# A two-layer graph network on one core: a ring of eight chunks, and the edge MLP, products, transposes and clearing rearranged

## The chip, the cores and the metric

The kernel runs on 1 core of one Trainium2 chip. The metric is the device time in microseconds (us); lower is better. Each kernel was executed three times, and the median counts. One more execution was taken by the hardware profiler; its page and trace are what is read here.

## The reference

12500 nodes with 32 features each; 212500 edges, sorted by destination, each with a source, a destination, 32 edge features and 4 spherical coefficients.

```python
h = relu(layernorm(x))
x = x + gcn(h)            # h * norm_src, gather by src, sum by dst, * norm_dst, @ weight + bias, relu
h = relu(layernorm(x))
x = x + edge_layer(h)

def edge_layer(node_attr):                     # MUL = 8
    h = relu(edge_feat @ W1 + b1)              # [e,32] @ [32,64]
    w = (h @ W2 + b2).reshape(e, 4, 8, 8)      # [e,64] @ [64,256]
    s, v = node_attr[:, :8], node_attr[:, 8:].reshape(n, 8, 3)
    s_e, v_e = s[src], v[src]
    m0 = ALPHA * (einsum('ei,eio->eo', s_e * sh0, w_000) + C110 * einsum('eim,em,eio->eo', v_e, sh1, w_110))
    m1 = ALPHA * (einsum('ei,em,eio->eom', s_e, sh1, w_011) + einsum('eim,eio->eom', v_e * sh0, w_101))
    return segment sums of m0, m1 by dst + SI_SCALE * (s @ si_w0, v by si_w1)
```

## The kernel before

Edges are cut into chunks of 1024 (CHUNK: eight tiles of 128), 208 chunks in all. Both layers run over all chunks. Buffers of a chunk lie in a ring of RING = 4 slots (idx, sh, ef, and g for the gathered rows), and every engine's loop body covers one turn of the ring. The order on each engine is written out by hand, and semaphores tie the engines together.

The first 32 chunks (EARLY) are gathered from x_rows while VectorE and TensorE count degrees by one-hot products (L743, L501). Then table1 is written, and GpSimd gathers the other 176 chunks from it, eight indirect DMAs a chunk (L351), one for each tile.

Layer 1 (`beside_early`, then `alone`): a chunk's gathered rows are multiplied on TensorE with a one-hot of the destinations (`segment_sums`, L517) into a window of 68 columns, which VectorE adds into acc_a (`add_sums`, L800). In `beside_early`, a unit of the early chunks stands beside each two others; it goes from TensorE to VectorE and back for the source norms (L542, L862). In `alone`, once per ring turn (j == LOOK) `next_block` finishes a block of 512 nodes if its sums are complete: `mid_block` stages them (L918), multiplies by the weight (L572), normalizes, and ScalarE stores the rows to table2. There are 25 blocks. GpSimd may refill a slot once VectorE has made a one-hot that stands three units on (L788).

Between the layers, TensorE transposes all blocks (L591), four at a time, for ScalarE to copy into acc_b; GpSimd has cleared acc_b (L385) and VectorE clears acc_a (L952).

Layer 2 (`layer2`, `steps`, `products`): per chunk, TensorE makes the hidden layer in two halves of 512 edges (`hidden`, L610), ScalarE applies relu (L455) and the coefficients (`coefs`, L467), TensorE makes 256 weights per edge (`weights`, L622) into four PSUM banks, and VectorE multiplies weights by coefficients (L981, L986, L992), sums part of them (L997), finishes the messages (L1006), adds the sums of the chunk before (L800), and makes the next one-hot. TensorE sums the messages (L517). SyncE's loop waits, per chunk, for `hidden_psum`, then `gathered`, then `messages_ready`, and issues ef, idx and sh for four chunks ahead. GpSimd waits for idx and for the slot:

```python
over_iterations(pool, lambda i: gather(
    i, table2, i + ITERS, lambda c, j: wait(pool, d_ready, c - RING + 1)))
```

VectorE's order in layer 2 is: products(c, 1), join_sums(c - 1), finish_messages(c), d_coefs(c + 1), products(c + 1, 0).

## Time and profile before

| what | value |
|---|---|
| device time, median of 3 | 5982.73 us (5958.65 to 6010.7) |
| profiled execution, span from first to last instruction | 5914.9 us |
| the profiled execution's own device time | not listed; only its span is |
| mean granted TensorE clock | 0.696 of full |
| TensorE matmul / VectorE / ScalarE / GpSimd busy | 3299.9 / 2809.8 / 710.4 / 3294.7 us |

PE is TensorE, PEld its weight loads, DVE VectorE, ACT ScalarE, POOL GpSimd, SP SyncE. A timeline row is start in us, length in us, engine, line, operation, what it writes and reads, and in brackets the idle time of the engine ahead of it with what ended it. "remote" says that the release came from something that the profile can't name; "issue" that the engine waited for nothing that the profile shows. Times of single instructions are in ns in the tables of groups.

### The profile page before, as it was taken

Reading aid. Unit: us, or ns where it says so; the run is one execution under the profiler, and the core shown is the slowest. Engines: PE = TensorE matmul, PEld = TensorE weight load, DVE = VectorE, ACT = ScalarE, POOL = GpSimd, SP = SyncE. Lnnn points to the kernel's source line nnn. Section 1 sums busy time; section 2 is a strip of 40 time slices with the busy share of each in tenths; the row PEclk is TensorE's granted clock in tenths of the full one; section 3 lists DMA queues with packets and bytes.
Section 4 is the critical chain, followed back from the end, with each engine's and each line's share of the span. In section 5 each row is a group of like instructions: output and inputs, shape, how many; then the busy total and the mean of one; then the engine's idle time right before and its main releaser. Section 6 shows DMA issues by size and latency. Waiting matters only on the chain.

```text
span 5914.9 us, 64171 instructions
## 1 busy us (share of the span) xinstructions
PE 3299.9 (56%) x17022; PEld 2418.7 (41%) x17023; DVE 2809.8 (48%) x4667; ACT 710.4 (12%) x2399; POOL 3294.7 (56%) x3337
## 2 busy tenths in 40 slices
PE   7943333321112112111587877677878777787877
PEld 5733333321111111111355555454555555555545
DVE  7743333321111111111466666666666666666666
ACT  0000000000000000000322222222222222222222
POOL 7775555555555455566555555555555555555453
PEclk9996555555555555555778777878777777777787
DMA  1011111110000000000111111111111111111110
GB/s 41 11 32 28 30 28 28 31 21 11 11 11 11 10 11 11 11 11 11 20 21 20 20 20 20 20 21 20 20 20 20 20 19 20 20 19 20 19 20 14
DMA packets 224089, 113.87 MB, mean 19 GB/s; under 512 B 148848, under 2 KB 212145, under 8 KB 223953
## 3 DMA queue, kind: packets, MB, share of 16 engines
q0 software_dynamic: 106496, 54.74, 7.0%
q1 hardware_dynamic: 106281, 39.22, 3.0%
q10 hardware_dynamic: 11280, 19.53, 1.0%
q8 instruction: 15, 0.25, 0.0%
q14 instruction: 17, 0.14, 0.0%
HBM read 108.30 MB, written 4.92 MB: 19 GB/s over the span
## 4 chain that ended last, share of the span: by engine, by line
another core or an unknown queue 33%; PE 32%; issue 15%; DVE 8%; POOL 5%; DVEq 4%; ACT 2%; DMA 0%; ACTq 0%; POOLq 0%
PE ps L622 12%; PE ps L517 10%; PE ps L610 6%; POOL g L351 5%; DVEq L805 2%; PE ps L542 1%; DVEq L804 1%; ACT q L467 1%; PE ps L572 1%; PE ps L658 1%; PE ps L660 1%; ACT hid L455 1%; DVE prod_b L981 1%; DVE msg_b L997 1%
## 5 line engine op out<-in xcount | busy, mean ns | idle before, releaser
L351 POOL DMA_INDIRECT g<-table,idx x3072 | 2971.2, 967 | 2479.6 <-issue 922.9
L622 PE MATMUL ps<-w_s,hid 128*128 128x256 f32 x3328 | 1110.6, 487 | 365.6 <-ACT hid L455 322.0
L622 PEld LDWEIGHTS ps<-w_s,hid 128*128 128x128 f32 x3328 | 761.5, 241 | 932.0 <-issue 406.3
L800 DVE TENSOR_TENSOR acc_a<-acc_a,ps 33x68 f32 (+1 forms) x416 | 91.2, 219 | 2201.0 <-remote 1949.1
L997 DVE TENSOR_REDUCE msg_b<-prod_b 128x128 f32<-128x1024 f32 x416 | 827.2, 1989 | 0.0
L517 PE MATMUL ps<-onehot,g 128*33 128x68 f32 x2816 | 340.0, 310 | 558.4 <-DMA g<-table,idx 296.1
L610 PE MATMUL ps<-ef,w_s 32*64 32x512 f32 x832 | 543.9, 734 | 42.2 <-issue 36.9
L455 ACT ACTIVATE hid<-ps,b_s 64x512 f32<-64x512 f32 x416 | 283.1, 681 | 2357.7 <-remote 1153.8
L517 PEld LDWEIGHTS ps<-onehot,g 128*33 128x33 f32 x2816 | 302.1, 170 | 587.1 <-issue 309.5
L981 DVE TENSOR_TENSOR prod_b<-ps,q 128x768 f32<-128x768 f32 x416 | 395.5, 951 | 274.8 <-remote 196.7
L517 PEld LDWEIGHTS ps<-onehot,prod_a 128*128 128x128 f32 x3328 | 455.1, 212 | 41.6 <-issue 10.2
L572 PE MATMUL ps<-w_l_s,ef 33*128 33x33 f32 x200 | 51.9, 422 | 730.8 <-DVE ef L918 529.7
L517 PE MATMUL ps<-onehot,prod_a 128*128 128x68 f32 x3328 | 443.3, 292 | 9.9 <-DVE msg_b L1006 6.5
L517 PE MATMUL ps<-onehot,msg_b 128*56 128x68 f32 x3328 | 297.4, 237 | 193.8 <-issue 192.9
L467 ACT ACTIVATE q<-g,sh 128x32 f32<-128x32 f32 x1664 | 372.7, 309 | 0.0
L542 PE MATMUL ps<-norm_src,hid 128*128 128x100 f32 x512 | 119.5, 428 | 437.7 <-DVE hid L833 342.1
L351 POOL DMA_INDIRECT g<-x_rows,idx x256 | 310.0, 1211 | 79.8 <-issue 77.7
L572 PEld LDWEIGHTS ps<-w_l_s,ef 33*128 33x128 f32 x200 | 48.5, 324 | 737.0 <-DVE ef L918 534.1
L501 PE MATMUL ps<-acc_b 128*128 128x100 bf16 x1664 | 314.3, 370 | 34.2 <-DVE acc_b L743 34.2
L517 PEld LDWEIGHTS ps<-onehot,msg_b 128*56 128x56 f32 x3328 | 242.2, 139 | 218.7 <-issue 202.5
L788 DVE TENSOR_TENSOR onehot<-iota_all,dst_rel 128x544 f32<-128x544 f32 x416 | 300.2, 722 | 52.0 <-issue 29.9
L430 ACT ACTIVATE root<-stat 128x4 f32<-128x4 f32 x50 | 10.3, 206 | 2412.9 <-DVEq L694 2412.9
(108 smaller groups left out, 2343.7 us busy)
## 6 DMA issues: line engine op xcount, KB each, us to landing
g<-table,idx POOLq DMA_INDIRECT x3072
ef<-edge_t SPq DMA_DIRECT2D x208, 128.0 KB, 2.3
ef<-src_rows ACTq DMA_DIRECT2D x31, 512.0 KB
idx<-src_chunks SPq DMA_DIRECT2D x416, 4.0 KB
g<-x_rows,idx POOLq DMA_INDIRECT x256
sh<-sh_chunks SPq DMA_DIRECT2D x208, 16.0 KB
table<-hn ACTq DMA_DIRECT2D x1, 1600.0 KB
table<-hn ACTq DMA_DIRECT2D x25, 64.0 KB
```

Of the source, the lines that this page charges most:

```text
L351: pool.indirect_dma_start(out=g[:, j, t, 0:FEAT], out_offset=None, in_=table, in_offset=bass.IndirectOffsetOnAxis(ap=idx[:, j, t:t + 1], a ...
L455: act.activation(hid[0:HID, h, :], ps[0:HID, H_BANK + h, :], ACT.Relu, bias=b1_s[:, 0:1]).then_inc(hidden_ready, 1)
L467: act.activation(q[:, j % 2, t, 8:40], g[:, j, t, 0:FEAT], ACT.Copy, scale=sh[:, j, t, 0:1])
L501: mm = pe.matmul(deg, oh_p[:, b, :, t], oh_r[:, b, :, t], start=False, stop=False, skip_group_check=True)
L517: mm = pe.matmul(ps[0:m, S_BANK + b, col:col + WIN], r, oh(t), start=(t == 0), stop=(t == TILES - 1))
L542: mm = pe.matmul(ps[:, W_BANK + t // 4, NR * (t % 4):NR * (t % 4 + 1)], early_p[:, P * t:P * (t + 1)], norm_src[:, :], start=True, stop=True)
L572: mm = pe.matmul(mid_ps[:, r, :], by_column(staged1)[:, r, :], w_l0_s[:, :], start=True, stop=True)
L610: pe.matmul(ps[0:HID, H_BANK + h, :], w1_s[32 * j:32 * j + 32, :], ef[32 * j:32 * j + 32, 512 * h:512 * h + 512], start=True, stop=True, t ...
L622: mm = pe.matmul(w_ps[h][:, t, :], hid[:, h, P * t:P * t + P], w2_s[:, :], start=True, stop=True)
L788: dve.tensor_tensor(onehot[:, b, :, :], iota_all[:, None, 0:WIN].to_broadcast([P, TILES, WIN]), dst_rel[:, bass.ds(c * TILES, TILES)][:, : ...
L981: dve.tensor_tensor(prod_b[:, h, :, 0:3, :].rearrange("p t m (i o) -> p t m i o", o=MUL), w[:, :, 128:192].rearrange("p t (i o) -> p t i o ...
L997: dve.tensor_reduce(msg_b[:, b, 4 * h:4 * h + 4, 0:32].rearrange("p t (g o) -> p t g o", o=MUL), prod_b[:, h, :, :, :].rearrange("p t g (i ...
```

## The change

The ring has eight slots, so each loop body covers eight chunks and there are 26 turns instead of 52; blocks are looked for at two places in a turn (LOOKS), and four early chunks stand beside eight others. Layer 2's slot is free for GpSimd after the last product of its chunk. The hidden layer is one product per chunk of 64 rows with a block-diagonal W1 (two edges' features above each other, 128 output rows). The weight products have 64 rows each, alternately in the upper and the lower half of the array; b2 comes in by bf16 products of ones with b2 split into three bf16 parts. W2's last two groups are stored transposed so that the summed index of the products lies innermost, and ScalarE writes the v coefficients already repeated (vq). VectorE makes one coefficient itself and finishes messages ahead of `join_sums`. The transposes go into `mid_block`; acc_a is cleared block by block there, and acc_b by VectorE in layer 1. SyncE's loop over early chunks now waits for all of them before it loads bounds and first sources.

```diff
-RING = 4
+RING = 8
+EARLY_PER = 4
+LOOKS = (1, 5)
...
-            with sp.Fori(0, EARLY_ITERS - 1) as i:
+            with sp.Fori(0, EARLY_ITERS) as i:
                 load1(i)
...
-            pool.wait_ge(added1, A_UNITS)
-            pool.memset(acc_b[:, :], 0.0).then_inc(acc_b_clear, 1)
...
-                i, table2, i + ITERS, lambda c, j: wait(pool, d_ready, c - RING + 1)))
+                i, table2, i + ITERS, lambda c, j: wait(pool, weights_used, 2 * (c - RING + 1))))
...
                 act.wait_ge(table2_ready, b + 1)
-                act.dma_start(block_rows(table2, b), block_columns(hn, b)).then_inc(table2_out, 16)
+                act.dma_start(block_rows(table2, b), hn_b).then_inc(table2_out, 16)
+                act.wait_ge(table2_out, 16 * b + 16)
+                act.wait_ge(turned, b + 1)
+                act.activation(by_column(acc_b[64:96, bass.ds(b * BLOCK, BLOCK)]),
+                               turn_ps.rearrange("f (r p) -> f r p", p=P), ACT.Copy).then_inc(staging_free, 1)
...
-                act.wait_ge(hidden_psum, 2 * (RING * i + j) + h + 1)
-                act.activation(hid[0:HID, h, :], ps[0:HID, H_BANK + h, :], ACT.Relu,
+                act.wait_ge(hidden_psum, RING * i + j + 1)
+                act.activation(hid[:, j % 2, :], ps[:, H_BANK + j % 2, :], ACT.Relu,
                                bias=b1_s[:, 0:1]).then_inc(hidden_ready, 1)
...
-                    act.activation(q[:, j % 2, t, 8:40], g[:, j, t, 0:FEAT], ACT.Copy, scale=sh[:, j, t, 0:1])
-                act.activation(q[:, j % 2, :, 40:48], g[:, j, :, 0:MUL], ACT.Copy).then_inc(coefs_ready, 1)
+                    ins = act.activation(
+                        vq[:, j % 2, t, :].rearrange("p (m o i) -> p m o i", m=3, i=MUL),
+                        g[:, j, t, MUL:FEAT].rearrange("p (m i) -> p m i", m=3)[:, :, None, :].to_broadcast(
+                            [P, 3, MUL, MUL]), ACT.Copy, scale=sh[:, j, t, 0:1])
+                ins.then_inc(coefs_ready, 1)
...
             def steps(i):
                 for j in range(RING):
-                    relu(*after(i, j, 1), 1)
+                    relu(*after(i, j, 2))
                     coefs(*after(i, j, 1))
-                    relu(*after(i, j, 2), 0)
...
                 mm.then_inc(mid_ready, 1)
+                pe.wait_ge(table2_ready, b + 1)
+                for r in range(BR):
+                    mm = pe.transpose(turn_ps[:, P * r:P * r + P], hn_b[:, r, :], ident[:, :])
+                mm.then_inc(turned, 1)
...
+                pe.matmul(ps[:, H_BANK + j % 2, :], w1_s[k:k + HID, :], ef[k:k + HID, j // 2, :],
+                          start=True, stop=True, tile_position=(k, 0)).then_inc(hidden_psum, 1)
...
-                for t in range(4):
-                    mm = pe.matmul(w_ps[h][:, t, :], hid[:, h, P * t:P * t + P], w2_s[:, :], start=True, stop=True)
+                for h in range(2):
+                    k = HID * h
+                    pe.matmul(ps[:, W_BANK + 2 * n + h, :], ones_b[k:k + HID, :], bias3[k:k + HID, :],
+                              start=True, stop=False, tile_position=(k, 0))
+                for u in range(2):
+                    for h in range(2):
+                        k = HID * h
+                        at = P * (2 * n + u)
+                        mm = pe.matmul(w_ps[n][:, 2 * h + u, :], hid[k:k + HID, j % 2, at:at + P],
+                                       w2_s[k:k + HID, :], start=False, stop=(u == 1), tile_position=(k, 0))
...
-                    hidden(*half(i, j, 3))
-                    weights(*half(i, j, 2))
-                    hidden(*half(i, j, 4))
-                    weights(*half(i, j, 3))
+                    hidden(*after(i, j, 2))
+                    weights(*after(i, j, 1), 0)
+                    weights(*after(i, j, 1), 1)
...
-                dve.tensor_copy(staged1, acc_a[0:FEAT + 1, bass.ds(b * BLOCK, BLOCK)]).then_inc(mid_go, 1)
+                sums = acc_a[0:FEAT + 1, bass.ds(b * BLOCK, BLOCK)]
+                dve.tensor_copy(staged1, sums).then_inc(mid_go, 1)
+                dve.wait_ge(mid_go, b + 1)
+                dve.sem_inc(sums_staged, 1)
+                dve.tensor_copy(sums, acc_b[0:FEAT + 1, 0:BLOCK]).then_inc(acc_a_clear, 1)
...
+            dve.memset(acc_b[0:64, :], 0.0).then_inc(acc_b_clear, 1)
...
-                dve.wait_ge(coefs_ready, c + 1)
+                dve.wait_ge(gathered[j], GATH * (i + ITERS + 1))
+                dve.wait_ge(sh_in[j], 16 * (i + 1))
+                dve.tensor_tensor(q[:, b, :, MUL:2 * MUL], g[:, j, :, 0:MUL],
+                                  sh[:, j, :, 0:1].to_broadcast([P, TILES, MUL]), ALU.mult)
...
                     msg_b[:, b, 4 * h:4 * h + 4, 0:32].rearrange("p t (g o) -> p t g o", o=MUL),
-                    prod_b[:, h, :, :, :].rearrange("p t g (i o) -> p t g o i", o=MUL),
+                    prod_b[:, h, :, :, :].rearrange("p t g (o i) -> p t g o i", i=MUL),
                     AX, ALU.add).then_inc(reduced, 1)
...
                     products(c, j, 1)
-                    if j == LOOK:
+                    finish_messages(c, j)
+                    if j in LOOKS:
                         final = final_blocks(dve, c - 1)
                     if not first:
                         join_sums(c - 1, 1 - b, *limits)
-                    finish_messages(c, j)
```

## Rows read from the trace of the kernel before

**Rows 1.** The first line of the profile's page.
```profile
span 5914.9 us, 64171 instructions
...
```

**Rows 2.** Stretches: us; PE, PEld, DVE, ACT, POOL busy us (instructions); clock, DMA share, GB/s.
```profile
...
391.00:1266.00 875.00, 279.26 (x1951) 261.30 (x1952) 265.11 (x519) 0.42 (x1) 496.78 (x513) 0.60 0.13 29
1266.00:2784.00 1518.00, 277.62 (x2043) 249.01 (x2042) 244.85 (x841) 9.46 (x46) 850.16 (x896) 0.52 0.08 11
2885.00:5914.00 3029.00, 2387.66 (x11189) 1639.59 (x11187) 1984.73 (x2978) 655.46 (x2274) 1590.13 (x1629) 0.77 0.11 20
...
```

**Rows 3.** Groups of layer 2, forms apart: count, busy us, mean ns, idle before.
```profile
...
L622 PE MATMUL ps<-w_s,hid 128*128 128x256 f32 x3309 | 1104.1, 487 | 365.6 <-ACT hid L455 322.0 <-issue 40.8 <-DVE prod_a L992 0.7
L997 DVE TENSOR_REDUCE msg_b<-prod_b 128x128 f32<-128x1024 f32 x415 | 825.2, 1989 | 0.0
...
L610 PE MATMUL ps<-ef,w_s 32*64 32x512 f32 x824 | 538.0, 733 | 42.2 <-issue 36.9 <-DVE prod_a L992 4.4
...
L467 ACT ACTIVATE q<-g,sh 128x32 f32<-128x32 f32 x1655 | 370.7, 309 | 0.0
...
L455 ACT ACTIVATE hid<-ps,b_s 64x512 f32<-64x512 f32 x412 | 280.4, 681 | 2351.4 <-remote 1153.8 <-PE ps L610 1039.1 <-issue 158.3
...
```

**Rows 4.** Waits in layer 2: us in total, times, longest.
```profile
...
ACT hid L455 <- remote: 1153.8, 118, 23.5
...
POOL g L351 <- DMA idx<-src_chunks: 748.3, 110, 11.8
...
DVE acc_a L800 <- remote: 465.4, 90, 11.6
...
```

**Rows 5.** Timeline of layer 2, a held stretch: start, us, instruction, idle before.
```profile
...
4060.39 1.01 PE L610 MATMUL ps<-ef,w_s 32*64 32x512 f32 x2 [0.74 <-issue]
...
4065.76 0.94 POOL L351 DMA_INDIRECT g<-table,idx  x1 [0.30 <-issue]
4069.00 0.68 ACT L455 ACTIVATE hid<-ps,b_s 64x512 f32<-64x512 f32 x1 [15.90 <-remote]
4069.06 0.23 DVE L800 TENSOR_TENSOR acc_a<-acc_a,ps 128x68 f32 x1 [9.13 <-remote]
...
4073.93 0.94 POOL L351 DMA_INDIRECT g<-table,idx  x1 [7.23 <-DMA idx<-src_chunks]
...
```

**Rows 6.** Timeline of layer 2, VectorE in a free stretch.
```profile
...
4093.05 0.35 DVE L1006 TENSOR_TENSOR msg_b<-msg_b,sh 128x192 f32<-128x192 f32 x1
...
4102.41 0.34 DVE L1006 TENSOR_TENSOR msg_b<-msg_b,sh 128x192 f32<-128x192 f32 x1
...
```

**Rows 7.** Timeline of layer 1, behind the early chunks.
```profile
...
1825.37 0.95 POOL L351 DMA_INDIRECT g<-table,idx  x1 [0.30 <-issue]
1830.32 0.22 DVE L800 TENSOR_TENSOR acc_a<-acc_a,ps 33x68 f32 x1 [33.99 <-remote]
1830.98 0.42 DVE L918 COPY ef<-acc_a 33x512 f32 x1 [0.44 <-DVE acc_a L800]
...
1842.51 0.94 POOL L351 DMA_INDIRECT g<-table,idx  x1 [16.19 <-DVE onehot L788]
...
```

**Rows 8.** Line L860: duration in ns, min/median/max.
```profile
...
L860 DVE TENSOR_REDUCE q<-prod_b x32: 985/986/987, 452.2 to 1298.8; 128x8 f32<-128x800 f32 x32
...
```

**Rows 9.** Timeline of the seam between the layers.
```profile
...
2818.54 1.89 PE L591 MATMUL ps<-ident,hn 128*32 128x128 f32 x8 [7.27 <-DVEq L938]
...
2821.45 10.78 DVE L952 MEMSET acc_a<- 128x12868 f32 x1 [3.02 <-issue]
...
2822.47 0.95 POOL L351 DMA_INDIRECT g<-table,idx  x1 [25.18 <-DMA table<-hn]
...
2872.58 3.67 PE L610 MATMUL ps<-ef,w_s 32*64 32x512 f32 x4
...
```

**Rows 10.** Waits from 36 to 345 us, where the degrees are counted.
```profile
...
DVE acc_b L743 <- PE ps L501: 90.2, 101, 0.9
...
```

**Rows 11.** DMA queues of the page: packets, MB, share of 16 engines.
```profile
...
q8 instruction: 15, 0.25, 0.0%
...
```

More of the change, by code:

```diff
@@ L154, in gnn_program @@
         early_mean = flat_q[:, TILES * (FEAT + 2):TILES * (FEAT + 3)]
+        flat_a = prod_a[:, :, :, :].rearrange("p b t k -> p (b t k)")
+        bias_raw, bias_left = flat_a[0:1, 0:HALF], flat_a[0:1, HALF:2 * HALF]
+        bias_parts = [flat_a[0:1, (4 + k) * (HALF // 2):(5 + k) * (HALF // 2)].bitcast(BF16) for k in range(3)]
         early_x = flat_q[:, TILES * (FEAT + 3):TILES * (2 * FEAT + 3)].rearrange("p (t f) -> p t f", f=FEAT)
@@ L583, in _ @@
             other_blocks(pe, blocks1, mid_block)
-            pe.wait_ge(table2_ready, BLOCKS)
-            for n in range(-(-NR // 4)):
-                wait(pe, turned_used, n - 1)
-                for r in range(4 * n, min(NR, 4 * n + 4)):
-                    k = (r - 4 * n) * P
-                    mm = pe.transpose(ps[0:32, S_BANK + n % 2, k:k + P], hn[:, r, :], ident[:, :])
-                mm.then_inc(turned, 1)
-            def half(i, j, ahead):
-                j, h = j + ahead // 2, ahead % 2
-                return i + j // RING, j % RING, h
@@ L599, in beyond, with after, hidden @@
-            def beyond(i, j, h):
+            def after(i, j, n):
+                return i + (j + n) // RING, (j + n) % RING
+            def beyond(i):
                 return isinstance(i, int) and i >= ITERS
-            def hidden(i, j, h):
-                if beyond(i, j, h):
+            def hidden(i, j):
+                if beyond(i):
                     return
-                k = 2 * (RING * i + j) + h
-                if h == 0:
-                    pe.wait_ge(ef_in[j], 16 * (i + 1))
-                wait(pe, hidden_ready, k - 1)
-                pe.matmul(ps[0:HID, H_BANK + h, :], w1_s[32 * j:32 * j + 32, :],
-                          ef[32 * j:32 * j + 32, 512 * h:512 * h + 512], start=True, stop=True,
-                          tile_position=(32 * j, 0)).then_inc(hidden_psum, 1)
@@ new lines, in hidden, with weights @@
+                wait(pe, hidden_ready, c - 1)
+                pe.matmul(ps[:, H_BANK + j % 2, :], w1_s[k:k + HID, :], ef[k:k + HID, j // 2, :],
+                          start=True, stop=True, tile_position=(k, 0)).then_inc(hidden_psum, 1)
+            def weights(i, j, n):
+                if beyond(i):
+                    return
+                c = RING * i + j
+                pe.wait_ge(hidden_ready, c + 1)
+                wait(pe, weights_used, 2 * c + n - 1)
+                for h in range(2):
+                    k = HID * h
+                    pe.matmul(ps[:, W_BANK + 2 * n + h, :], ones_b[k:k + HID, :], bias3[k:k + HID, :],
+                              start=True, stop=False, tile_position=(k, 0))
+                for u in range(2):
+                    for h in range(2):
+                        k = HID * h
+                        at = P * (2 * n + u)
+                        mm = pe.matmul(w_ps[n][:, 2 * h + u, :], hid[k:k + HID, j % 2, at:at + P],
+                                       w2_s[k:k + HID, :], start=False, stop=(u == 1), tile_position=(k, 0))
@@ L946, in _ @@
             dve.wait_ge(table1_out, 16)
+            dve.wait_ge(bias_in, 16)
+            dve.memset(acc_b[0:64, :], 0.0).then_inc(acc_b_clear, 1)
+            dve.tensor_scalar(w2_s[:, 0:64], w2_s[:, 0:64], float(ALPHA * C110), None, ALU.mult)
+            dve.tensor_scalar(w2_s[:, 64:256], w2_s[:, 64:256], float(ALPHA), None, ALU.mult)
+            dve.tensor_scalar(sel_b_s[64:96, :], sel_b_s[64:96, :], float(SI_SCALE), None,
+                              ALU.mult).then_inc(weights_scaled, 1)
+            dve.wait_ge(acc_b_clear, 1)
+            two = bias_raw.rearrange("a (u w) -> a u w", w=256)
+            dve.tensor_scalar(two[:, :, 0:64], two[:, :, 0:64], float(ALPHA * C110), None, ALU.mult)
+            link(dve.tensor_scalar(two[:, :, 64:256], two[:, :, 64:256], float(ALPHA), None, ALU.mult))
+            left = bias_raw
+            for k in range(3):
+                link(dve.tensor_copy(bias_parts[k], left))
+                if k < 2:
+                    link(dve.tensor_tensor(bias_left, left, bias_parts[k], ALU.subtract))
+                    left = bias_left
+            dve.sem_inc(bias_split, 3)
             with dve.Fori(A_ITERS, REG_ITERS - 1) as i:
@@ L951, in _ @@
             other_blocks(dve, blocks1, mid_block)
[L952 to L957 removed]
+            dve.wait_ge(acc_a_clear, BLOCKS + 1)
             def d_coefs(i, j):
@@ L1100 @@
     w2 = np.concatenate([np.asarray(L1_gnn_W2), np.asarray(L1_gnn_b2)[None, :]])
-    w2 = np.concatenate([w2[:, 3 * mm:], w2[:, :mm], w2[:, 2 * mm:3 * mm], w2[:, mm:2 * mm]], axis=1)
+    turn = [w2[:, k * mm:(k + 1) * mm].reshape(-1, MUL, MUL).transpose(0, 2, 1).reshape(-1, mm) for k in (2, 1)]
+    w2 = np.concatenate([w2[:, 3 * mm:], w2[:, :mm], *turn], axis=1)
+    w1 = np.zeros((2, 2, FEAT, 2, HID), np.float32)
+    w1[:, 0, :, 0, :] = np.asarray(L1_gnn_W1)
+    w1[:, 1, :, 1, :] = np.asarray(L1_gnn_W1)
     skip = np.zeros((FEAT, FEAT), np.float32)
```

194 lines of the change are left out of this document (98 added, 96 removed).

## The prediction, made before the change was run

> **What bounds the kernel now.** I read the stretches first, then the groups of layer 2, its waits, and two stretches of its timeline. Layer 2 takes 3029.0 of the 5914.9 us [rows 1, 2]. It has 208 chunks, so a chunk costs 14.56 us. No engine is busy that long: in the same row TensorE is busy 2387.7 us (11.5 a chunk), VectorE 1984.7 (9.5), ScalarE 3.2 a chunk, and GpSimd issues eight gathers of 0.95 us with 0.30 between them, 8 x 1.25 = 10.0 us a chunk [rows 2, 5]. So handovers set the pace. The held stretch shows which: TensorE's hidden-layer product begins at 4060.39 and takes 1.01 us, yet ScalarE, which waits for it, starts at 4069.00; VectorE's add of sums, held 9.13 us, starts at 4069.06. Both begin 2.3 us after GpSimd's last gather of the burst ended (4065.76 + 0.94) [rows 5]. In layer 1 the same: last gather ends 1826.3, the add starts 1830.32 after 33.99 us [rows 7]. So TensorE's signals reach the others late while a long burst of gathers runs. Waits marked "remote" are of this kind: 1153.8 us at ScalarE, 465.4 at VectorE's add [rows 4]. After the release, VectorE must finish messages, SyncE must load indices, and only then does GpSimd go on, 7.23 us after its last gather; such waits for indices are 748.3 us, 3.6 a chunk [rows 4, 5]. Where nothing is held, a chunk takes 4102.41 - 4093.05 = 9.4 us, VectorE's own work [rows 6]. It isn't gathers alone that hold TensorE: while the degrees are counted they run too, and VectorE's longest wait for TensorE there is 0.9 us [rows 10]. The mechanism is not shown, only its coincidence with bursts behind that stage.
>
> **Layer 2, part by part.**
> VectorE: the sum of the products, 2 a chunk, takes 1.99 us for 1024 elements read at a stride of eight floats. The change packs the summed index innermost. A packed sum of 800 elements takes 0.986 us [rows 8], 1.23 ns an element, so 1024 take at most 1.26. Saved: 2 x 0.73 = 1.5 us a chunk. The three product instructions keep their element counts, so I cost them at nothing. One multiplication of 64 elements is added, between 0.1 and 0.35 us; I take 0.2. VectorE: 9.5 - 1.5 + 0.2 = 8.2 us.
> TensorE: the hidden products, two of 32 rows a chunk, become one of 64. L610 is busy 538.0/208 = 2.6 us a chunk; half goes, 1.3. The weight products stay eight of 256 columns, but on 64 rows, alternating between the upper and lower half of the array. L622 is busy 1104.1/208 = 5.3 us [rows 3]; if two halves run together 2.65 goes, if not nothing. I take 1.5, since the trace has no pair. Four bf16 bias products of 512 columns are added. Between nothing and 4 x 0.65 (a busy L610 instruction, 538.0/824) = 2.6; I take 1.3, the middle, because a bf16 product is one instruction where an fp32 one is two (824 instructions for 416 products) [rows 3]. TensorE: 11.5 - 1.3 - 1.5 + 1.3 = 10.0, between 7.6 and 12.8.
> The Trainium skill, "TensorEngine Tiling (Array Packing)", section Key Properties, has tiles loading and multiplying in parallel, but a drain at each change of tiling mode. By the first TensorE would have 8.9 us, by the second about what it has now; no row shows either.
> ScalarE: one relu of 128 rows replaces two of 64, each 681 ns. The eight copies grow from 32 to 192 elements: by the slope from 309 ns at 32 to 681 at 512, 433 ns each [rows 3]. Beside a small copy that goes, about +1 us a chunk, and -0.7 from the relu. It stays under 4.5 us and has VectorE's 8 us of cover; without that cover it would cost 1 us a chunk, 208 us.
> Order: VectorE now finishes messages of chunk c before it waits for the sums of c-1. Behind the held add used to stand the messages, behind them SyncE's index load and TensorE's own sums. Also the relu now comes a whole chunk ahead of its use, where it used to be a half. ScalarE still waits for the relu ahead of the coefficients, so that hold remains.
> The ring: with eight slots the indices lie ready, so the 3.6 us a chunk of index waits go. What is late next is the slot. The rule changes from the vsh sum to the last product of the chunk, but seven chunks back instead of three. GpSimd's bursts thereby close up, which is what holds TensorE.
> The pace: a burst of k chunks lasts 10.0k us. Then 2.3 us until signals come, then VectorE needs between a third of a chunk and a whole one (2.7 to 8.2 us) to free a slot; I take 5.3. For k = 2 a chunk costs (20 + 7.6)/2 = 13.8, for k = 3 12.5. VectorE works 8.2 us a chunk, and the first 6 to 9 us of a burst are free as in rows 6. I take 12.9 us. Layer 2: 208 x (14.56 - 12.9) = -345 us. The bounds are GpSimd's 10.0 to 10.4 us below, and above no gain at all.
>
> **The seam.** The transposes take from 2818.54 to 2872.58, 54 us, and go into the block steps of layer 1 [rows 9]. Their cover in layer 1 is GpSimd, which is not delayed by them. What is late next is the gather: it starts at 2822.47, and a first chunk needs 10.0 us. Net -54 + 10 = -44 us. The clearing of acc_a (10.8 us, at 2821.45) already lay beside the transposes; without its move it would now cost 10.8.
>
> **Layer 1.** It is 875 + 1518 us [rows 2]. Behind the early chunks the cycle is a burst of 32 gathers (four slots, 40 us) plus 16.19 us until VectorE frees a slot [rows 7]. With eight slots TensorE finds more data ready when it is released. If five chunks pass a cycle instead of four, (50 + 16.2)/5 = 13.2 us against 14.05, -0.8 over some 112 chunks, -90 us; if still four, nothing. I take -60. Against it: a block step gains one copy of 33 x 512 (0.42 us, as its staging copy [rows 7]) with a link, 25 x 0.7 = 17 us; TensorE waits in each for the whole block before it may sum the next chunk, beside GpSimd, 0 to 60 us, I take 15. Clearing acc_b moves from GpSimd to VectorE, 10.8 us as acc_a's took [rows 9], with scalings and splitting some 6 more one time. SyncE's bounds and first sources now stand behind all 32 early chunks, not 28: 4 x 10.0 = 40 us later, most of it beside gathers that run anyway; 0 to 40, I take 12. Sum: -60 + 17 + 15 + 17 + 12 = 0, between -120 and +90.
>
> **Sum.** -345 - 44 + 0 = -389: span 5914.9 - 389 = 5526. The median of the runs, 5982.73, stands 67.8 us above the profiled span; the profiled execution's own time isn't listed, so I carry this difference unchanged: 5594, say 5590 us.
>
> **Rivals.**
> Gather pace: if shorter TensorE work and the looser order let the free stretches persist (9.4 us already beside nearly continuous gathers, rows 6), layer 2 runs at 10.4: 208 x 4.16 = -865, with the seam 5074 us. For it: a 9.4 us chunk exists. Against: layer 1's holds, where TensorE has little to do and still waits 34 us. Chance 0.17.
> Longer holds (the other side): no index wait breaks the bursts, k goes to 4. A cycle is 40 us, 2.3, then VectorE may do in the free 9 us one chunk and must do three of 8.2 behind, of which about 8 us lie in the next burst: 40 + 2.3 + 17 = 59.3, 14.8 a chunk, +50 us; the early stage, with its handovers to and fro for each early chunk, has 32 of them, each held by one such 2.3 us more, 875 + 70, and the seam gives 44 back: 6059 us. It decides from the point where bursts of 32 gathers are the rule in layer 2. For it: rows 7. Chance 0.11.
> Code: the loop bodies double. If they no longer stay in the engines' buffers, each turn fetches. The instruction queue with the larger packets carries 15 in the whole run [rows 11], fewer than the 52 turns, so now the loops' turns fetch nothing there. Price: 25 turns of layer 2 with a hold like the 7.23 to 9.13 us of rows 5, +180 to 230: 5800 us. Chance 0.12.
> The Trainium skill, "Runtime: NRT & Kernel Launch", section Instruction fetch mechanics, says that a taken branch out of the current two-page window stalls for a fetch. By that the present loops should fetch too; rows 11 speak against it.
> Only engine work counts: ring and order give nothing, VectorE's 1.3 us a chunk are -270, seam -44: 5670; part of the forecast's own spread.
>
> **How the numbers follow.** Forecast 0.60 (5300 to 5800), gather pace 0.17, code 0.12, longer holds 0.11. Likeliest: 5590. To hold 8 in 10 the range runs from 5170 to 5900: all of the forecast and the code case, and the upper part of the gather-pace case. The three runs lie within 0.9% of one another, so 1% is about what can be told from no change. Faster by over 1% (under 5923) 0.87, within 1% 0.05, slower 0.08.
>
> **What would show it.** In the profile after: the packed sum at 1.2 us; the weight products' busy time well under 5 us a chunk if halves pair; index waits gone from GpSimd's rows, slot waits in their place; bursts of 16 to 24 gathers in layer 2 with remote waits behind them; layer 2 beginning at about 2840 plus layer 1's change; few instruction packets. I am wrong if bursts are long and a chunk still costs 14 us or more, if TensorE is busy over 13 us a chunk, or if the holds vanish.

## The result and the profile after

The changed kernel took 6079.48 us (median of 4 runs, 6073.26 to 6092.49) against 5987.74 us for the old one (median of 4 here): ratio 1.017, 95% interval 1.012 to 1.022. It is slower by 1.2 to 2.2%; 5590 was forecast, with a range from 5170 to 5900. A second comparison, in another job (a job is one session of runs on one chip), gave 6064.29 against 5885.63, ratio 1.030 (1.026 to 1.034).

The page of the changed kernel, its span, the engines' busy time and the two instruction queues [rows 1, 11]:

```profile
span 6080.2 us, 63715 instructions
...
PE 3107.2 (51%) x17438; PEld 2423.4 (40%) x17439; DVE 2534.7 (42%) x4908; ACT 771.2 (13%) x1983; POOL 3251.2 (53%) x3334
...
q14 instruction: 207, 1.69, 0.1%
q8 instruction: 29, 0.48, 0.0%
...
```

Its stretches: early chunks, rest of layer 1, seam, layer 2 (columns as in rows 2):

```profile
391.00:1280.00 889.00, 262.27 (x1828) 245.15 (x1829) 256.20 (x502) 0.42 (x1) 492.30 (x513) 0.59 0.14 28
1280.00:2670.00 1390.00, 282.13 (x2196) 250.89 (x2193) 282.29 (x899) 34.08 (x69) 846.54 (x889) 0.55 0.09 13
2670.00:2740.00 70.00, 24.90 (x156) 19.02 (x156) 23.64 (x78) 7.68 (x17) 20.98 (x23) 0.60 0.13 25
2743.00:6072.00 3329.00, 2217.64 (x11572) 1656.59 (x11570) 1700.06 (x3178) 714.46 (x1861) 1578.84 (x1647) 0.66 0.10 18
```

Layer 2 takes 3329.0 us for 208 chunks, 16.0 us a chunk where it was 14.56 [rows 2], though VectorE is busy only 1700.06/208 = 8.2 us a chunk and TensorE 10.7. So everything lost lies in layer 2, and in waiting. The layer even begins earlier than it did. Timeline of the seam, against rows 9:

```profile
2720.48 2.08 PE L597 MATMUL ps<-ef,w_s 64*128 64x512 f32 x4
...
2722.01 0.95 POOL L350 DMA_INDIRECT g<-table,idx  x1 [42.61 <-DMA table<-hn]
...
```

The first hidden product comes at 2720.48, not 2872.58, and the first gather at 2722.01, not 2822.47. By the first of these, layer 1 and seam gave 152 us. Layer 2 from there to the span's end took 3359.7 us where it took 3042.3: +317. The sum is the +165 us between the two spans.

Groups of layer 2 (rows 3 are their counterparts) and its waits (rows 4):

```profile
L615 PE MATMUL ps<-w_s,hid 64*128 64x256 f32 x3298 | 897.0, 495 | 421.2 <-issue 414.4
...
L463 ACT ACTIVATE vq<-g,sh 128x192 f32<-128x192 f32 x1656 | 594.3, 446 | 6.5 <-issue 6.5
...
L1011 DVE TENSOR_REDUCE msg_b<-prod_b 128x128 f32<-128x1024 f32 x414 | 501.2, 1211 | 0.0
...
L597 PE MATMUL ps<-ef,w_s 64*128 64x512 f32 x410 | 331.4, 896 | 21.7 <-issue 21.6
L609 PE MATMUL ps<-bias,ones_b 64*128 64x512 bf16 x824 | 315.8, 484 | 200.5 <-issue 122.7 <-DVE prod_a L1006 75.7
```
```profile
ACT hid L451 <- remote: 2079.1, 100, 88.4
DVE acc_a L794 <- remote: 1159.5, 89, 64.0
POOL g L350 <- DVE prod_a L1006: 1126.9, 100, 21.8
```

The instructions cost about what was forecast. The waits don't: ScalarE's remote wait went from 1153.8 to 2079.1 us, VectorE's from 465.4 to 1159.5, and where GpSimd waited 748.3 us for indices it waits 1126.9 for a slot. One cycle of the changed kernel, out of its timeline (as rows 5):

```profile
4168.62 0.95 POOL L350 DMA_INDIRECT g<-table,idx  x1 [11.72 <-DVE prod_a L1006]
...
4176.83 0.97 PE L597 MATMUL ps<-ef,w_s 64*128 64x512 f32 x1
...
4177.02 0.36 DVE L1020 TENSOR_TENSOR msg_b<-msg_b,sh 128x192 f32<-128x192 f32 x1
...
4185.28 0.27 PE L510 MATMUL ps<-onehot,prod_a 128*128 128x68 f32 x1 [1.64 <-issue]
...
4187.41 0.27 PE L510 MATMUL ps<-onehot,prod_a 128*128 128x68 f32 x1 [1.85 <-issue]
4187.70 0.95 POOL L350 DMA_INDIRECT g<-table,idx  x1 [0.30 <-issue]
...
4191.73 0.69 ACT L451 ACTIVATE hid<-ps,b_s 128x512 f32<-128x512 f32 x1 [23.46 <-remote]
4191.79 0.23 DVE L794 TENSOR_TENSOR acc_a<-acc_a,ps 128x68 f32 x1 [14.41 <-remote]
...
4199.41 0.68 DVE L1006 TENSOR_TENSOR prod_a<-ps,q 128x512 f32<-128x512 f32 x1
...
4200.90 0.95 POOL L350 DMA_INDIRECT g<-table,idx  x1 [12.25 <-DVE prod_a L1006]
```

Sixteen gathers run from 4168.62 to 4188.65. Some ten us in, TensorE drops to an instruction every 0.7 to 2 us, for no cause that the profile shows ("issue"). Such a stretch, together with the late signals at its end, is called a hold below. The hidden product that ScalarE waits for ended at 4177.80; ScalarE starts at 4191.73, 3.1 us behind the last gather. VectorE had stopped at 4177.38. Then 9.1 us pass until GpSimd starts again (4191.79 to 4200.90): VectorE works its way to the product that frees a slot. 20.0 + 3.1 + 9.1 = 32.2 us for two chunks, 16.1 each.

### The profile page after: what moved, and what is told of

Its sections match the earlier page's. It is cut to its first block, busy times and chain, and to the rows that moved or that the text cites. A ratio compares the mean times of both kernels' runs of the same rounds, so it can differ in the third digit from the quotient of the medians.

```text
span 6080.2 us, 63715 instructions
## 1 busy us (share of the span) xinstructions
PE 3107.2 (51%) x17438; PEld 2423.4 (40%) x17439; DVE 2534.7 (42%) x4908; ACT 771.2 (13%) x1983; POOL 3251.2 (53%) x3334
## 4 chain that ended last, share of the span: by engine, by line
another core or an unknown queue 35%; PE 22%; issue 22%; DVE 9%; DVEq 5%; ACT 4%; POOL 4%; DMA 0%; ACTq 0%; POOLq 0%
PE ps L510 10%; PE ps L615 5%; ACT vq L463 4%; POOL g L350 4%; PE ps L597 2%; DVE prod_b L996 2%; DVEq L799 2%; PE ps L535 2%; DVEq L798 2%; DVE msg_b L1011 1%; PE ps L609 1%; PE ps L565 1%; DVE prod_a L1006 1%; DVE prod_b L1000 1%
## 5 line engine op out<-in xcount | busy, mean ns | idle before, releaser
L350 POOL DMA_INDIRECT g<-table,idx x3072 | 2941.3, 957 | 2660.3 <-DVE prod_a L1006 1126.9
L615 PE MATMUL ps<-w_s,hid 64*128 64x256 f32 x3328 | 903.7, 496 | 421.2 <-issue 414.4
L510 PE MATMUL ps<-onehot,prod_a 128*128 128x68 f32 x3328 | 626.2, 341 | 411.1 <-issue 399.1
L615 PEld LDWEIGHTS ps<-w_s,hid 64*128 64x128 f32 x3328 | 591.4, 246 | 613.2 <-issue 571.2
L510 PEld LDWEIGHTS ps<-onehot,prod_a 128*128 128x128 f32 x3328 | 587.8, 258 | 544.4 <-issue 508.1
L463 ACT ACTIVATE vq<-g,sh 128x192 f32<-128x192 f32 x1664 | 597.2, 446 | 15.8 <-DMA g<-table,idx 9.3
L996 DVE TENSOR_TENSOR prod_b<-ps,vq 128x768 f32<-128x768 f32 x416 | 396.4, 953 | 382.3 <-ACT vq L463 180.9
L1011 DVE TENSOR_REDUCE msg_b<-prod_b 128x128 f32<-128x1024 f32 x416 | 503.7, 1211 | 0.0
L451 ACT ACTIVATE hid<-ps,b_s 128x512 f32<-128x512 f32 x208 | 143.0, 688 | 2593.4 <-remote 2079.1
L609 PE MATMUL ps<-bias,ones_b 64*128 64x512 bf16 x832 | 318.3, 486 | 211.8 <-issue 133.1
L597 PE MATMUL ps<-ef,w_s 64*128 64x512 f32 x416 | 334.5, 897 | 21.7 <-issue 21.6
```

The costliest lines, as they stand in the source:

```text
L350: pool.indirect_dma_start(out=g[:, j, t, 0:FEAT], out_offset=None, in_=table, in_offset=bass.IndirectOffsetOnAxis(ap=idx[:, j, t:t + 1], a ...
L451: act.activation(hid[:, j % 2, :], ps[:, H_BANK + j % 2, :], ACT.Relu, bias=b1_s[:, 0:1]).then_inc(hidden_ready, 1)
L463: ins = act.activation(vq[:, j % 2, t, :].rearrange("p (m o i) -> p m o i", m=3, i=MUL), g[:, j, t, MUL:FEAT].rearrange("p (m i) -> p m i" ...
L510: mm = pe.matmul(ps[0:m, S_BANK + b, col:col + WIN], r, oh(t), start=(t == 0), stop=(t == TILES - 1))
L597: pe.matmul(ps[:, H_BANK + j % 2, :], w1_s[k:k + HID, :], ef[k:k + HID, j // 2, :], start=True, stop=True, tile_position=(k, 0)).then_inc( ...
L609: pe.matmul(ps[:, W_BANK + 2 * n + h, :], ones_b[k:k + HID, :], bias3[k:k + HID, :], start=True, stop=False, tile_position=(k, 0))
```

## The experiments

Each run is compared with the old kernel on the same chip in the same job. Runs of different jobs are best compared by ratio, since the old kernel itself took 5886 to 5988 us in the jobs with holds. The "pace" is my own figure, in us a chunk: start of the first gather of layer 2's chunk 192 less that of chunk 16, over 176. A burst ends where GpSimd gathers nothing for 1.5 us. The last two columns are for bursts of 16 gathers: how many of all bursts of these chunks they are, and VectorE's busy time inside one (mean, us; a burst is 20 us long). The last four rows come from jobs in which nothing was held (below).

```
run               us       before   ratio (95%)            pace   bursts of 16   VectorE in one
before            5987.7   -        -                      14.67  37 of 126      13.3
changed (2nd)     6064.3   5885.6   1.030 (1.026..1.034)   15.92  80 of 96       9.1
r1_ring4          5955.0   5885.6   1.011 (1.008..1.015)   15.67  69 of 107      8.8
f1_slot           5717.5   5897.1   0.969 (0.964..0.973)   14.24  60 of 116      11.0
f2_order          5855.9   5897.1   0.992 (0.988..0.995)   15.04  74 of 101      9.7
f3_nobias         6134.2   5897.1   (one run)              16.46  88 of 88       8.8
g4_slot_order     5797.3   5982.5   0.969 (0.967..0.972)   14.48  64 of 106      10.7
r1_pause1         5371.6   5897.1   0.910 (0.906..0.914)   12.66  0              -
g2_before_pause   5524.5   5982.5   0.923 (0.920..0.926)   12.60  0              -
g1_best           5293.3   5982.5   0.884 (0.882..0.886)   12.76  0              -
h1_memset2        5302.5   5895.4   0.898 (0.894..0.901)   12.71  0              -
h2_memset1        5228.5   5895.4   0.886 (0.882..0.889)   13.04  0              -
h3_every2         5542.7   5895.4   0.940 (0.935..0.945)   13.83  66 of 110      11.2
e1_ring4          4354.9   4372.8   0.996 (0.994..0.997)   10.24  no gap at all  -
e2_pause1         4863.5   4372.8   1.112 (1.110..1.114)   12.64  0              -
e2_pause2         5380.4   4372.8   1.231 (1.228..1.233)   15.18  0              -
h4_mixed          5020.1   4374.1   1.148 (1.146..1.150)   12.22  0              -
```

**First job: another state of the machine.** The ring of four, with everything else as changed:

```diff
-RING = 8; EARLY_PER = 4; LOOKS = (1, 5)   # and twelve UNITS
+RING = 4; EARLY_PER = 2; LOOKS = (1,)     # six UNITS
```


> The changed kernel with the ring set back to four chunks (two early chunks to a turn, one look for a finished block); products, bias, order of VectorE's steps, transposes and clearing stay as changed. Long bursts: with four slots the index loads again break up GpSimd's work in layer 2, as before the change, and VectorE keeps its 8.2 us a chunk: 13.3 to 14.2 us a chunk in layer 2 and 5600 to 5800 us. Code: the loop bodies halve, so the second queue's instruction packets fall from 207 to some 20 and the kernel again comes to 5600 to 5900 us; this run can't part the two. Products, bias or order at fault: 15.5 us a chunk or more in layer 2, 6000 us or more.

It took 4354.86 us, but the old kernel beside it took 4372.83 instead of some 5900: in this job nothing was held. Waits of e1_ring4 in layer 2:

```profile
ACT hid L450 <- PE ps L596: 586.0, 202, 9.0
POOL g L349 <- issue: 491.4, 1612, 0.3
```

No remote wait is left, and GpSimd gathers through layer 2 without a gap of 1.5 us. So whether there are holds depends on a state of the machine: the old kernel is the same program in both. It isn't a matter of the chip either: a chip on which the old kernel took 5885.63 us in one job had it at 4374.06 in a later one (h4_mixed's). What sets the state I don't know. Without holds e1_ring4 stands at GpSimd's 10.2 us a chunk and is 0.4% faster than the old kernel. The changed kernel itself was never caught there, and of the old one there is no trace without holds.

> The changed kernel; in layer 2 GpSimd stores one row of 32 floats by a DMA of its own into a scratch row ahead of each chunk's gathers, and waits until it has landed (some 2 us in which it gathers nothing). Long bursts: no burst of 16 is left without a gap; if a gap of 2 us lets TensorE's signals out, a chunk takes 12 to 13.5 us and the kernel 5250 to 5550 us; if the gap must be as long as the 3.1 us seen behind a burst, little changes. Code: GpSimd's pause changes nothing in the loops' back edges, 6080 us or more, up to 6500 if every pause adds to the chain (208 x 2 us).

> The same with two such small DMAs one behind the other ahead of each chunk's gathers, some 4 us. Long bursts: the gap is longer than the 3.1 us seen behind a burst, so every chunk's signals get out; a chunk takes 13 to 14.5 us, 5450 to 5800 us. Code: 6080 to 6900 us.

The edit of e2_pause1, in short (the two lines stand in layer 2 only):

```diff
 for j in range(RING):
+    pool.dma_start(scratch, x_rows[0:1, :]).then_inc(paused, 16)
+    pool.wait_ge(paused, 16 * (RING * i + j + 1))
     pool.wait_ge(idx_in[j], 16 * (iteration + 1))
```

With no holds to break, the pauses only cost: the pace is 12.64 and 15.18 us, and the time 491 and 1008 us over the old kernel's. These runs decide nothing on bursts. (e2_pause2 has two such pairs.)

**The ring, under holds.** c1_after is the changed kernel once more, the table's second row.

> The changed kernel, unchanged. In the runs just before, the old kernel took 4373 us, not the 5988 us beside which the changed one was first timed, and the remote waits were gone from the traces: whether TensorE's signals are held depends on more than the kernel. If this run falls where they are held, the changed kernel again takes 6080 us and the ratio is again 1.01 to 1.02. If it falls where they are not, GpSimd's gathers set the pace of both layers (10.0 to 10.3 us a chunk) and only the seam's 44 us and what the block steps cost in layer 1 are left: 4320 to 4345 us against 4373, ratio 0.988 to 0.994. Code fetch would show there as 25 turns of 3 us: 4400 us or more.

> The changed kernel with the ring of four once more, beside the changed kernel itself on one chip. Where signals are held: long bursts expects 5600 to 5800 us, products, bias or order at fault 6000 us or more. Where they are not held: 4355 us as before, and the changed kernel within 1% of it, since the ring can't speed up a GpSimd that never waits.

Now the holds were there. Ring four came to 5955.04, in neither of the two ranges: 109 us better than ring eight, still 69 worse than the old kernel. Its pace is 15.67, and bursts of 16 are the rule there too (69 of 107). So my first theory, that the ring makes the long bursts, fell. Of layer 2's loss of 1.25 us a chunk (14.67 to 15.92) the other edits hold 1.00 and the ring 0.25; in the whole kernel, where the other edits also bring their gain in layer 1, the ring costs 109 of the 179 us. Some 26 us of that lie ahead of layer 2, whose first gather starts at 2691 us with ring four and at 2717 with ring eight. Code fetch is part of it at most, as far as nothing that the ring gives hides it: with ring four the second instruction queue carries 18 packets, with ring eight 206, and what the two differ by in layer 2 is 0.25 us a chunk, 52 us. With ring eight VectorE stands 2.7 to 3.3 us, once in most turns of eight chunks and for no cause that the profile shows (19 times in the changed kernel's first trace, chunks 16 to 192), with ring four once in all; that alone is some 55 us.

**Gathers, or GpSimd's DMAs at this pace?** Layer 2's eight gathers a chunk become eight plain DMAs of 128 consecutive rows; the messages come from the wrong nodes.

```diff
+    pool.dma_start(g[:, j, t, 0:FEAT], table[P * t:P * t + P, :]).then_inc(gathered[j], 16)
```


> The changed kernel with layer 2's gathers left out: each of the eight of a chunk is replaced by a plain DMA of GpSimd's of 128 consecutive rows, so the messages come from the wrong nodes. Long bursts of gathers at fault: the remote waits of ScalarE and VectorE (2079 and 1160 us) go almost wholly and a chunk takes 8.5 to 10.5 us, VectorE's own work, 4600 to 5000 us. Code or the order at fault: the waits stay and a chunk takes 14 us or more. If plain DMAs of GpSimd's hold TensorE as gathers do, nothing changes.

> Layer 2's gathers replaced by plain DMAs of GpSimd's once more (the messages come from the wrong nodes), on a chip with holds if this is one. If the indirect gathers hold TensorE: layer 2 takes 8.5 to 10.5 us a chunk as on the chip without holds, 4650 to 5000 us in all, layer 1 unchanged. If any close row of GpSimd's DMAs holds it: 14 us a chunk or more, 5600 us or more.

Without holds 4139.36 us, with them 4662.01. In layer 2 both run at the same 9.3 us a chunk (VectorE's finished messages, chunk 16 to 192); the difference is layer 1, whose gathers were left in (layer 1's last chunk starts at 2671 us for 2178, so the holds were there). Waits of r1_plain in layer 2, under holds:

```profile
ACT hid L454 <- PE ps L600: 1185.8, 205, 12.9
POOL g L351 <- DVE prod_a L1009: 937.7, 193, 8.9
```

No remote wait is left, so without the gathers the holds are gone. But the run doesn't part the kind of DMA from the length of the burst. A plain DMA keeps GpSimd busy for 548 ns where a gather takes 957, so eight of them are through in 4.2 us, and GpSimd then waits 4.9 us for the slot (937.7/193): its bursts are short and broken by pauses longer than those that end the holds below. Whether plain DMAs in a row of 20 us would hold TensorE wasn't tried.

**The slot's release, VectorE's order, TensorE's queue.**

The edit of f1_slot, in short:

```diff
+    act.activation(s8[:, j % 2, :, :], g[:, j, :, 0:MUL], ACT.Copy)    # ahead of the vq copies
-    g[:, j, tiles, None, 0:MUL]  ...  wait(pool, weights_used, 2 * (c - RING + 1))
+    s8[:, b, tiles, None, :]     ...  wait(pool, coefs_ready, c - RING + 1); wait(pool, d_ready, c - RING + 1)
```


> The changed kernel with the slot given back earlier: ScalarE copies the eight scalar features of a chunk first, VectorE's last product reads the copy, and GpSimd waits for ScalarE's copies and VectorE's vsh sum of seven chunks back, as before the change, not for the last product. Late slot at fault (GpSimd's 12.25 us gap is mostly VectorE's way to that product): the gap falls to 7 us and a chunk costs 14 us or less, 5650 us or less. Catch-up at fault (VectorE must do what it was held from, whenever GpSimd starts): the gap shrinks, but the next hold takes as much, 5950 to 6080 us. On a chip without holds no change (within 0.5% of the changed kernel).

The edit of f2_order, in short:

```diff
-    finish_messages(c, j)
     ...
     join_sums(c - 1, 1 - b, *limits)
+    finish_messages(c, j)
```


> The changed kernel with VectorE's old order: it waits for the sums of chunk c-1 and adds them before it finishes the messages of chunk c. If the new order is what costs layer 2 its 200 us against the ring of four: 5850 to 5900 us. If the order is as harmless as it looked: 6040 to 6100 us. Forecast of the old prediction (the new order helps): 6100 us or more.

> The changed kernel without its bias products (the edge MLP's second bias is left out). In holds TensorE issues one instruction in some 0.7 us. If the length of its queue sets when the signals come, four products and four weight loads fewer a chunk take 1 to 3 us of each chunk: 5500 to 5850 us. If not, 6000 us or more. Without holds: no change.

> The changed kernel with early slot and old order together, no pause. The slot alone gave 345 us and the order 208. If they mend different parts of the catch-up they add up: 5510 us (13.3 us a chunk in layer 2). If both only move the point at which GpSimd starts again, the two together give no more than the slot: 5680 to 5730 us. The catch-up theory, which has every hold cost what VectorE could not do, expects little of the second: 5600 to 5720 us.

The slot alone takes 5717.45 us (347 less than the changed kernel's 6064 in the job before), the old order alone 5855.87 (208 less). Both together give the same 0.969 of the old kernel as the slot alone. So they don't add up: the second has nothing left to mend. The slot's 5717 lies between what late slot (5650 or less) and catch-up (5950 or more) expected: part of the gap only moved. The table shows what the slot does. In the changed kernel VectorE does 9.1 us of work in a burst of 20 and the rest in the gap, before GpSimd may start; with the early slot 11.0, in the old kernel 13.3. GpSimd starts the burst while VectorE still catches up.

What the order costs isn't the hold's end: TensorE's signals come 2.9 us after a burst in place of 3.0 (medians). It is the point at which the hold catches VectorE. Its waits in layer 2, c1_after and then f2_order:

```profile
DVE acc_a L794 <- remote: 1104.0, 88, 64.7
DVE prod_b L996 <- remote: 138.5, 22, 17.0
```
```profile
DVE acc_a L794 <- remote: 862.0, 80, 66.4
DVE prod_b L996 <- remote: 254.1, 46, 12.7
```

Held at the sums (acc_a), VectorE is 9.1 us away from the product that frees a slot, in both runs. With the old order it is as often held at the next chunk's first product (36 of the 74 bursts of 16, against 21 of 80 with the new order), 5.6 us away, and in f2_order the gap behind such a burst is 8.4 us (median) and not 12.1. Over all bursts of 16 the mean gap is 10.3 us for 12.2, 1 us a chunk, about the 0.88 by which the paces differ. Why the old order leads there more often, no run shows.

f3_nobias, a single run, has four products fewer a chunk and is no faster, with the signals again 3.0 us after a burst (median): the length of TensorE's queue doesn't look like what ends the hold. Waits of g4_slot_order: the index waits are back, GpSimd now outruns SyncE:

```profile
ACT hid L456 <- remote: 1234.0, 70, 88.0
...
POOL g L351 <- DMA idx<-src_chunks: 710.5, 97, 17.4
```

**Breaking the bursts.**

> The pause of 2 us ahead of each chunk's gathers once more. Its first run fell on a chip without holds, where it only cost 8 x 0.3 us a chunk of GpSimd's time. On a chip with holds: a cycle of the changed kernel there is a burst of two chunks (20 us), 3.1 us until TensorE's signals come, then 9 us until a slot is free, 16.0 us a chunk; VectorE gets some 7 to 9 us of its work done while a burst runs and is held for the rest. With bursts of one chunk nothing of the burst is left to hold: 12.3 to 13.5 us a chunk, 5300 to 5550 us. If the gap must be over 3 us to let signals out, 6000 us or more. On a chip without holds: 4860 us again.

> The old kernel with the same pause ahead of each chunk's gathers in layer 2. If the pause alone is the gain: 12.6 to 13.3 us a chunk, 5886 - 208 x 1.3 to 1.9, 5490 to 5620 us, and what the changed kernel has over it (5372) is its layer 1 and seam, some 150 us. If the old kernel's index waits or its 9.5 us of VectorE's work stand in the way: 5650 us or more. Without holds: 4373 + 468 = 4840 us.

> The changed kernel with the slot given back early (as f1_slot), VectorE's old order (as f2_order), and the pause of 2 us ahead of every chunk's gathers from table 1 and table 2, layer 1 too. Breaking the bursts is what counts, and with it GpSimd's own 10.2 us and the 2.3 us of the pause set the pace, 12.6 us a chunk in both layers: layer 1 behind the first 32 chunks 176 x 12.6 = 2220 us for 2267, layer 2 as in the paused run: 5300 to 5350 us. If slot and order give more beside the pause, under 5250 us; if pauses in layer 1 only cost, over 5372 us. Without holds: 4363 + (176 x 2.3) + 500, about 5250 us.

r1_pause1 is e2_pause1's program, now under holds. It takes 5371.61 us: 0.910 of the old kernel, where the same kernel without the 208 pauses took 1.030 of it. Its layer 2, waits and one pause in the timeline:

```profile
POOL g L355 <- DMA scratch<-x_rows: 411.1, 183, 3.0
ACT hid L456 <- remote: 235.6, 26, 10.0
...
```
```profile
4113.06 0.53 POOL L348 DMA_DIRECT2D scratch<-x_rows  x1
...
4116.30 0.98 POOL L355 DMA_INDIRECT g<-table,idx  x1 [2.71 <-DMA scratch<-x_rows]
```

ScalarE's remote wait falls from about 2000 to 235.6 us, and GpSimd, idle 2.7 us a chunk, sets the pace. The old kernel with the same pause runs at the same pace (12.60 against 12.66), so the change's own worth there is only layer 1 and the seam: layer 2's first gather starts at 2711 us, not 2878. Packed sum and ring give nothing there: GpSimd is the bound. g1_best adds slot, order and pauses in layer 1: 5293.33 us, 78 less. Its first gather of layer 2 starts 98 us earlier (2614), its pace is no better (12.76): slot and order add nothing beside the pause.

**How short, how idle, how often?** The pause of g1_best as a clearing of 2048 or 800 unused floats, or ahead of every second chunk:

```diff
-    pool.dma_start(scratch, x_rows[0:1, :]).then_inc(paused, 16)
+    pool.memset(flat_hn[0:1, 2 * BLOCK:2 * BLOCK + 2048], 0.0).then_inc(paused, 1)    # h2: 800
```


> As g1_best, with the pause filled: in place of the small DMA and its wait GpSimd clears 2048 unused floats of one partition, some 1.8 us by the old kernel's clearing (10.85 us for 12868). If it is enough that no gather is issued for 2 us: 12.2 us a chunk, 5180 to 5300 us. If GpSimd must be idle for TensorE to come through: bursts count on through the clearing and the kernel is back at 5750 us or more.

> The same with 800 floats, some 0.7 us. If any break ends what builds up over ten us of gathers: 11.1 to 11.5 us a chunk, 4950 to 5100 us, the best version. If the held signals need the 2 to 3 us seen behind a burst: holds come back, 5400 us or more.

> As g1_best with the DMA pause ahead of every second chunk only, so bursts are of 16 gathers (20 us) by construction. The catch-up theory has each hold cost what VectorE could not do in the burst: 20 + 2.3 and the rest of 16.4 us of work above the 7 to 9 us done in the burst, less what overlaps the pause: 13.5 to 15 us a chunk, 5550 to 5800 us, though it pauses half as much. If the pause mattered only by its sum: 11.5 us a chunk, under 5100 us.

> As h2_memset1 with two lengths: 800 floats cleared ahead of each chunk's gathers in layer 1, where the short break brought the first gather of layer 2 to 2452 us against 2633 with 2048 floats, and 1400 floats (some 1.3 us) in layer 2, where 800 let some holds back (13.04 us a chunk with 2.95 us between bursts) and 2048 did not (12.71). If the break needed in layer 2 lies between: 12.2 to 12.7 us a chunk, 5040 to 5150 us, ratio 0.86 to 0.875, the best of all. If nothing under 2 us ends them: 5200 us or more.

h1 clears for 1.80 us (mean of its rows) and has g1_best's pace (12.71 for 12.76) and time (5302 for 5293 us, in another job): GpSimd needn't be idle, only not gathering. From gather to gather its breaks are 2.7 us long (median). h2 clears for 0.76 us, 1.7 us from gather to gather. In layer 1 that is enough (first gather of layer 2 at 2452 us, as in h4_mixed with nothing to hold), in layer 2 some holds return:

```profile
ACT hid L461 <- remote: 1175.5, 92, 22.3
...
DVE acc_a L805 <- remote: 418.9, 96, 9.3
```

Even so h2 is 74 us faster than h1 beside it, by layer 1. h3, with half of g1_best's pauses, is 240 us slower than h1 beside it, and has bursts of 16 again (66 of 110): the length of the burst decides, not the sum of pauses. h4_mixed fell on the state without holds (5020 us for 4374), where its pauses are loss; whether its lengths are best under holds stays untested. By ratio g1_best and h2_memset1 (0.884 and 0.886, intervals overlapping) beat both kernels under holds; without holds e1_ring4 does, by 0.4%.

## Why the prediction was wrong

**The step that failed is the pace formula of layer 2**, burst 10.0k + 2.3 + 5.3 us, and in it the 5.3 us that VectorE was given to free a slot. The formula gave 13.8 us a chunk for k = 2; k was 2 (74 of 102 bursts have 16 gathers), and a chunk cost 16.0. Way to the slot: 9.1 us, not 5.3. Release: 3.1 us, not 2.3. I had taken "between a third of a chunk and a whole one" and its middle, while the slot rule that I had read in the diff, the last product instead of the vsh sum, puts it at the far end, 8.2 us, and a little beyond (VectorE waits 0.93 us for ScalarE's vq on the way). The trace of the old kernel would have told: behind its own bursts of 16 the median way is 4.9 us, so my 5.3 was the way of the old rule. f1_slot is the test: with the old rule the pace falls to 14.24, next to my 13.8, and the way to 4.4. The 2.3 us were read off one burst; the old kernel's median is 2.65. And the layer 1 stretch that was called "the same" has 4.0 us from the last gather's end (1826.3) to the add (1830.32). The formula has no term for what VectorE gets done inside the burst; the 6 to 9 us that I called free went only into the choice of 12.9 between 12.5 and 13.8. That work was 13.3 us in the old kernel and is 9.1 in the changed one.

**"Order" was counted as a help**, without a number, and costs 208 us alone, nothing beside the early slot.

**"Index waits go, the slot is late next"**: right (748.3 us gone, 1126.9 in its place), and the trade was a bad one: 5.4 us a chunk for 3.6. k = 3, which carried the forecast down to 12.9, hardly came in layer 2 (no burst of 24 among these chunks). So the ring's expected gain went into a later slot.

**Terms that held**: packed sum 1211 ns (at most 1.26 us forecast); VectorE 8.2 us a chunk (8.2); ScalarE's copies 446 ns (433). TensorE: forecast 10.0, measured 10.7; weights 897.0/208 = 4.3 us a chunk (5.3 - 1.5 = 3.8), bias 1.5 (1.3), hidden 1.6 (1.3). Under holds the alternating halves give 1.0 of the possible 2.65 us, at a granted clock of 0.66 (0.77 before). In e1_ring4, without holds, they give nearly all: the weight products are busy 630.1/208 = 3.0 us a chunk, 2.3 less, at a granted clock of 0.80, and TensorE as a whole is busy 8.7. The Trainium skill ("TensorEngine Tiling (Array Packing)", Key Properties) has parallel tiles and a drain at a change of mode. e1_ring4 agrees with the first, by which the forecast had 8.9 us; what a drain costs no run here tells. None of this mattered under holds, since engines weren't the bound.

**Seam and layer 1**: -44 and 0 forecast; from layer 1's last chunk of gathers to the first hidden product 98.0 us became 50.8 (-47), and that last chunk starts at 2669.7 in place of 2774.6 (-105). GpSimd reaches its 64th chunk from table 1 13 us later and gains 118 behind it. My "-90 for five chunks a cycle" comes near this number, but by luck: its mechanism isn't there. Behind the early chunks most cycles of the changed kernel still pass four chunks, as a burst of 24 gathers and one of 8, in 49 us where the old kernel took 56 for a burst of 32 (longer bursts, of 40, come only at the end):

```profile
1798.84 0.95 POOL L350 DMA_INDIRECT g<-table,idx  x1 [3.06 <-DVE onehot L782]
...
1834.84 0.94 POOL L350 DMA_INDIRECT g<-table,idx  x1 [5.78 <-DVE onehot L782]
...
1847.90 0.95 POOL L350 DMA_INDIRECT g<-table,idx  x1 [3.35 <-DVE onehot L782]
```

r1_ring4 has the same cycle of 24 and 8, 49 us long. So the gain in layer 1 isn't the ring's; which of the other edits splits the burst, no run shows.

**Device time**: I carried 67.8 us from span to median. In all runs since, the span is 1.8 us under its own execution's time; the 67.8 was the spread of the old kernel's runs, so from the profiled span the sum reads 5528.

**Rivals.** Longer holds named the sign, the place and nearly the number (6059 us), at 0.11; but by bursts of 32, which are not the rule in layer 2. Its mechanism, remote waits that grow, was right; its size (k) wrong. Code: packets rose from 17 to 207, and VectorE did get a stall of some 2.9 us a turn, a third of the 7.23 to 9.13 us of that rival: some 55 us. That it is a fetch isn't shown. Gather pace (5074, from 10.4 us a chunk) describes the state without holds, where e1_ring4's layer 2 does run at 10.24, but its layer 1 too, so 4355. The chances were wrong where they rested most: 0.87 for faster hung on a catch-up time that no row of the old kernel showed for the new slot rule. And no rival had a machine without holds.

## What to carry to other kernels

When two engines take turns, cost a cycle as burst plus gap, and work out the gap from the last instruction ahead of the new release point, not from the old one: a deeper buffer released later can be slower. Where signals arrive only behind bursts, shorten the bursts; a deliberate break of some 2.7 us for each 10 us of gathers in layer 2 took 8% off the old kernel and, by the two ratios, 12% off the changed one, more than all edits of the change together cost. When a substitute is to tell one kind of work from another, see that it keeps the length and the spacing of the work as well. And run the old kernel in each job: the same program took 4373 or 5900 us, and a fix for the one state costs 11 to 15% in the other.

## What the hardware showed that I had not expected

- Under holds, TensorE goes down to about 0.7 matmuls a us from ten us into a burst of GpSimd's indirect gathers on (median of the 74 bursts of 16 in the changed kernel; 11572 in 3329 us, 3.5 a us, over all of layer 2), and its results become known to others 2.6 to 3.1 us behind the burst's end (ScalarE's start, medians of the runs). A break every eight gathers takes this off the path: with breaks of 2.7 us between gathers GpSimd sets the pace, and ScalarE's remote waits are 236 to 823 us in place of 1154 and 2079; 1.7 us were enough in layer 1, not in layer 2. Eight plain DMAs a chunk show no hold, but their bursts last only 4.2 us.
- The state lasts a whole job (the 7 to 13 runs of the old kernel in a job lie within 1.4%, but for one of 4616 us beside seven of 4367 to 4378) and can change on one chip between jobs. Gathers take the same time in both (970 ns without holds, 957 with).
